# One inner loop of two turns over the parity of the edge pair, in place of two copies of the node program

## The reference

```
x = layernorm(x + gcn(x))    # 3 layers: segment_sum(norm * (h@W)[src], dst) + b, + x0, relu, batchnorm
x = layernorm(x + eve(x))    # 2 layers: p = relu(h@Wpool+b); max and min of p[src] over dst,
                             #   relu(w0*max + w1*min + b) @ Weve + h @ Wself + bias
x = layernorm(x + sage(x))   # 2 layers: mean of h[src] over dst @ Wl + b + h @ Wr, silu between
x = layernorm(x + gat(x))    # leaky_relu(x[src]@Wl + x[dst]@Wr + e@We) . att, softmax over dst,
                             #   weighted sum of x[src]@Wl, gelu, + x, layernorm
```

## Time and profile before

| what | value |
|---|---|
| time, median of 3 runs | 16096.09 us (16064.56 to 16136.27) |
| profiled execution, its own time | 16116.22 us |
| its span | 16114.4 us |
| mean granted TensorE clock | 0.668 of full speed |
| instructions | 164866 |

### The profile page before, as it was taken

How to read it: one execution, slowest core, us unless ns; L and a number is a source line. 1 busy time by engine, 2 the same in 40 slices (tenths; PEclk the granted TensorE clock), 3 DMA queues, 4 the chain that set the end, 5 groups by cost and what they waited for, 6 DMA issues and landing times. The chain is left out here.

```text
span 16114.4 us, 164866 instructions
## 1 busy us (share of the span) xinstructions
PE 6150.8 (38%) x34202; PEld 5070.4 (31%) x34203; DVE 7076.3 (44%) x16762; ACT 4640.9 (29%) x8751; POOL 7665.0 (48%) x7679
## 2 busy tenths in 40 slices
PE   1025544555445540144444444333333333333332
PEld 0014443444444440133333333333323332122221
DVE  2223333433333349633334545222334443667676
ACT  1211111211111125322223333222223332555454
POOL 4554444455445443444554444444444444455553
PEclk6557776777677775566766767666666666666666
DMA  5965554666566667544445545445445553333232
GB/s 150 186 148 175 171 170 140 220 200 199 170 203 200 199 196 245 173 155 154 157 127 183 174 162 172 140 157 158 155 152 182 178 179 110 94 93 94 88 94 76
DMA packets 1864914, 2570.42 MB, mean 160 GB/s; under 512 B 255773, under 2 KB 1369141, under 8 KB 1864662
## 3 DMA queue, kind: packets, MB, share of 16 engines
q1 hardware_dynamic: 1235734, 1678.48, 34.2%
q10 hardware_dynamic: 403160, 513.66, 9.1%
q0 software_dynamic: 225792, 375.94, 8.4%
HBM read 1499.62 MB, written 1129.98 MB: 163 GB/s over the span
## 5 line engine op out<-in xcount | busy, mean ns | idle before, releaser
L989 POOL DMA_INDIRECT sums_gcn<-m_result,m_idx x1176 | 1267.0, 1077 | 2173.0 <-DVE m_result L1310 1837.1
L1572 DVE SCALAR_TENSOR_TENSOR m_acc<-m_n_out,m_scales,m_res_b 128x128 f32<-128x128 f32 (+1 forms) x2352 | 641.1, 344 | 2656.7 <-remote 1889.7
L1123 ACT ACTIVATE m_nodeT<-m_n_turn 128x512 f32<-128x512 f32 x980 | 571.3, 595 | 4279.8 <-PE m_n_turn L1096 2758.2
L989 POOL DMA_INDIRECT sums_eve<-m_result,m_idx x784 | 834.8, 1065 | 1550.7 <-DVE m_result L1398 1325.5
L1096 PE MATMUL m_n_turn<-k_ident,m_in_y 128*128 128x128 f32 x5488 | 1033.3, 336 | 1293.8 <-issue 609.8
L989 POOL DMA_INDIRECT sums_sage<-m_result,m_idx x784 | 775.5, 989 | 1522.2 <-DVE m_result L1310 1296.8
L981 POOL DMA_INDIRECT m_rows<-node_rows_a,m_idx x1176 | 1154.9, 982 | 339.5 <-issue 339.5
L1096 PEld LDWEIGHTS m_n_turn<-k_ident,m_in_y 128*128 128x128 f32 x5488 | 796.5, 174 | 1563.6 <-issue 747.1
L1108 PE MATMUL m_n_out<-k_sage_r,m_nodeT 128*128 128x128 f32 x3136 | 599.3, 366 | 1616.7 <-DVE m_z L1676 1226.0
L1108 PEld LDWEIGHTS m_n_out<-k_sage_r,m_nodeT 128*128 128x128 f32 x3136 | 556.2, 272 | 1644.8 <-issue 1644.8
L1517 PE MATMUL m_gram<-m_y 128*128 128x129 f32 (+1 forms) x4800 | 713.6, 298 | 713.1 <-issue 636.0
(11 more groups left out here) (290 smaller groups left out, 16997.6 us busy)
## 6 DMA issues: line engine op xcount, KB each, us to landing
sums_gcn<-k_gcn_b SPq DMA_DIRECT2D x291, 512.0 KB
m_in_sums<-sums_gcn SPq DMA_DIRECT2D x291, 512.0 KB
m_in_y<-node_rows_a SPq DMA_DIRECT2D x291, 512.0 KB
node_rows_a<-m_y ACTq DMA_DIRECT2D x194, 512.0 KB
m_in_x<-in_x_dram SPq DMA_DIRECT2D x194, 512.0 KB
m_in_y<-node_rows_b SPq DMA_DIRECT2D x194, 512.0 KB
sums_eve<-k_eve_b SPq DMA_DIRECT2D x194, 512.0 KB
m_in_sums<-sums_eve SPq DMA_DIRECT2D x194, 512.0 KB
```

Source lines behind the costliest of these rows:

```text
L989: pool.indirect_dma_start(self.node_sums[:, :], bass.IndirectOffsetOnAxis(self.idx[s][:, T + t:T + t + 1], 0), self.result[b][:, t, :], No ...
L1123: act.activation(out, src, ACT.Copy).then_inc(self.n_turn_read, 1)
L1572: ins = dve.scalar_tensor_tensor(out=self.acc[b][0:n, tt, :], in0=ph.node_out(i, n)[:, t, :], scalar=self.scales[b][0:n, tt:tt + 1], in1=s ...
```

## The change

The copies for both parities of an edge pair stay, in the two branches of an If inside an inner loop over the parity `par`; the node program stands once behind it. Its bounds and counts are computed from `par` and give the values that `slot_counts` gave. Engines without a node unit keep the old body. Nothing else is edited.

```diff
     with eng.Fori(2, full // 2) as q:
-        unit(0, q)
-        unit(1, q)
+        if node_unit:
+            with eng.Fori(0, 2) as par:
+                with eng.If(par < 1):
+                    edge_unit(2 * q, 0, q, 4, 4)
+                with eng.Else():
+                    edge_unit(2 * q + 1, 1, q, 4, 4)
+                nodes(ready(2 * q + par - 1), ready(2 * q + par), [q, q, q - 1 + par, q - 1 + par])
+        else:
+            unit(0, q)
+            unit(1, q)
     edge_unit(full, 0, full // 2, 2, 4)
```

## The result

| kernel | median | runs |
|---|---|---|
| before | 16096.43 us | 5 (16064.56 to 16139.23) |
| with the change | 16225.89 us | 5 (16200.0 to 16282.78) |

The ratio is 1.0074, 95% interval 1.0052 to 1.0096: the change costs 0.7%, some 119 us by the ratio. The profiled execution has a span of 16207.5 us against 16114.4, 93 us more, with a mean granted TensorE clock of 0.696 against 0.668; both kernels run at a mean near 0.67 or 0.70, and their times don't follow it. Forecast was 16115 us, no change (0.62), in a range of 16020 to 16220; slower had a chance of 0.23. By the ratio the kernel takes 16215 us, just inside the range, by its median 16226, just above it. The cost is six times the +19 us of the sum, and clear of noise.

The account below looks back on a forecast made before the run. It took waits between engines, a serial chain of POOL's run, nodes and edge program, as the bound. Control +30, gat's fetches -5 and other fetches -6 made +19 us on 16096: 16115 us, range 16020 to 16220.

Parts of the forecast that it names:

- Chain and place: Convolution loops: a serial cycle of POOL's run, nodes, edge program; control costs only between nodes and the first edge result.
- Counts nothing elsewhere: Control outside the stretch from last node work to first edge result, or on engines not last there, costs nothing.
- nothing beside it that could absorb a delay: The convolution cycle, 67.70 us a turn in eve1, was said to have no slack, so a delay lengthens it.
- (a): Added control in the convolution loops: 0.85 us a turn, 60 us if serial, half taken: +30 us, bounds 0 and +102.
- hardly tell: Gcn2's periods with and without a back edge differ by 0.27 us, the gap by 0.42; ground for taking half.
- Rival 3: Eve1-like loops: five more pairs in each of three phases fall into short periods, -60 us, about -90 in all; chance 0.17.
- sign of being wrong: Eve: a shift of the short periods by more than one in four would show the forecast wrong in sign.
- (b): Gat loop: one node program copy fewer ends the instruction fetches and DVE's stalls; -5 us, bounds 0 and -37.
- (c): Instruction fetches outside the loops, where phases begin and end: fewer with smaller loops; -6 us, bounds 0 and -22.
- Rival 2: SP's new control falls in POOL's run and delays its loads: +120 us in three phases, 16215 us; chance 0.05.
- the table loads: An added ACT table load of 1.28 us in each edge pair of four phases: +102 us, 16200 us; chance 0.04.

Follow-up runs that it names:

- A: Conditions of the first measurement and one later group of runs: the kernel before takes 16096 us, then 16061 us on that group's chip.
- B: Conditions of the other three groups of runs, each on its own chip: the kernel before takes 12200 to 12225 us.
- rotated_change: The change turned by half a step, shared nodes first, then the If with the edge programs, against the kernel before: ratio 0.9955, run in B.
- gat_only: Shared node program in the gat phase alone, other eight phases as before, against the kernel before: ratio 1.0004, run in B.
- dve_only: The changed loop on DVE alone, in all nine phases, against the kernel before: ratio 1.0035, run in A.
- again2: The kernel before once more, nothing changed, for a second profile in A: ratio 0.9999.
- again: The kernel before once more, with only an empty line added at the end of the file: ratio 1.0007, run in B.
- rotated: The kernel before with its loop body turned by half a step, back edge behind an edge program: ratio 0.9941, 12154 us against 12225, in B.
- rotated_mix: Loop turned by half a step: gat as in rotated_change, the other phases as in rotated, against the kernel before: ratio 0.9965, in B.

## Why the prediction was right and wrong

**The number.** The cost was forecast at +19 us and called the same; it is +119. The range held the result only at its edge.

**Chain and place: right in the main.** In A the cost comes with control between the nodes' last work and the edge program's first result: ACT's loop brings it in eve, DVE's in sage2. In gcn and sage1 the split is within the spread. SP and PE cost nothing in B. Two things were too strong. "Counts nothing elsewhere" fell in eve2 of rotated_change, and "nothing beside it that could absorb a delay" does not hold in gcn, where 0.60 us of gap became 0.2 to 0.4 us of period.

**(a), the size of the control: the step that failed.** I priced 0.85 us a turn and took half, +30 us. DVE's gap grew by 0.60 us a pair in gcn and 0.63 in sage2, and ACT's in eve1 by 0.4, so 0.8 to 1.2 us a turn; the loops grew by 0.80 us a pair on average, not 0.21. Two mistakes: I put all of it on one of the two transitions of a turn, though after the change both pass an inner loop end and the If (1.22 and 1.41 us against 0.51 and 0.93); and I halved it since two periods "hardly tell", when the halving had no more behind it than those two. Priced in full at 0.60 x 20 x 7 it is +84 us, against 112 at the measured 0.80 us a pair. Loop by loop the gap is a rough price all the same: gcn took less than it, eve1 and sage2 more than twice as much.

**Rival 3, short periods: right mechanism, wrong sign.** Eve1's short periods changed their kind, as named; but later control on ACT did away with all of them (some 16 of eve1's 29 us: four of 17 periods were 63.1 to 64.4 us, where most others were about 67.7) and made none. In sage2 later control on DVE did the same, for some 12 of its 23 us. The prediction gave this way round no price; it named it only as an "against" and as a sign of being wrong.

**(b), gat: wrong in two ways.** The fetches went in the change, but not because a copy was gone: gat_only has the same gat program and twice the packets. And their loss brought nothing in A: dve_only has no packets in gat and DVE's "issue" row there falls from 34.3 us to 13.9, yet the loop takes 1589.5 us against 1591.8 (again2). What a stall costs in B is open, as the clock moves gat's periods by as much. In A gat got slower with the change, by 42 and 58 us counted from sage2's loop, of which ACT's loop alone makes 17 and DVE's none (against again2). The table of waits in A hints where: ACT's wait for the layer norm's root from "remote" and "issue" grows from 30.7 + 46.9 to 79.4 + 61.4 us (again2, then change). A node program that starts later falls deeper into POOL's run. That is argued from the rows, no run isolates it. The rows are again2, then change.

```profile
ACT g_ln_root L479 <- issue: 46.9, 9, 11.7
ACT g_ln_root L479 <- remote: 30.7, 3, 13.1
```

```profile
ACT g_ln_root L479 <- remote: 79.4, 11, 16.8
ACT g_ln_root L479 <- issue: 61.4, 11, 15.6
```

**(c)** Packets outside the gat loop fell from 125 to 116; the stretches between the loops show no gain. No run prices this term. Rival 2 and the table loads did not come: SP's sums' load in eve1 stands 47.2 us behind the start of POOL's run, as in most pairs before, and ACT loads as many tables.

With (a) in full and the lost short periods of eve1 and sage2 the convolution loops come to 84 + 16 + 12, +112 us, which is what they took. The sum was put together afterwards and no run tests it. Gat's 42 to 58 us on top overshoot the measured 119; part of that may be what degrees gains, and the rest is not placed.

## What to carry to other kernels

In a loop whose engines hand one chain around, price control by the idle gap before the first instruction behind it, in every transition that passes it, and in full; then allow for less where the cycle has slack, and for more where a few periods are shorter than the rest and a small delay may lengthen them. Put loop ends where the engine waits anyway, and check by the profile that nothing waits for it there. A loop's instruction fetches are not told by the length of its text alone: count the packets in its stretch in every version. And before a gain is put down to lost fetches, compare the granted clock of the same stretches.

## What the runs showed of the hardware

- The same program took 12211 and 16061 us on two chips, each within 0.4%. On the slower one SP's register instructions at L864 last up to 0.71 us, on the faster one 0.19 at most. Why was not found. The change's cost in eve1 was 29 us on the one and 10 on the other (16 pairs), in sage2 23 and 0.
- A taken loop end lengthens the gap before the next instruction by 0.42 us on DVE (0.51 against 0.93 us in gcn2) and 0.45 on ACT (1.85 against 2.30 in eve1) where no instruction packets come with it. In gat, with packets, DVE's gaps are 3 to 9.3 us.
- In gat's loop in B, pairs behind a stretch at TensorE's full clock took 87.8 to 89.0 us, behind a mean of 0.80 to 0.93 they took 89.7 to 93.8 (again, rotated, rotated_change, rotated_mix), with the same data instructions.
- The same loop code had 0 (change) or 80 (gat_only) instruction packets in its stretch; what stood ahead of it differed.
- The inner loop end and the If together lengthen DVE's gap by 0.60 us a pair (0.72 to 1.32 in gcn2), though the branch instructions themselves last 47 to 62 ns.
